# Waiting for gate/up weights one group earlier, and a bias matmul moved to the head of its block

## The reference, cut to what matters

```python
xn = layernorm(x)                                   # x: (2, 16384, 1024) f32
u  = einsum('bld,ed->ble', xn, W_in) + b_in         # D = 1024
h_t = exp(lambda_log) * h_{t-1} + gamma * u_t       # scan over blocks of 2048 rows
s  = einsum('bld,ed->ble', h, W_out) + b_out + xn
gate, up = xn @ (w_gate/127).T, xn @ (w_up/127).T   # hidden size 3072
f  = (silu(gate) * up) @ (w_down/127).T
out = x + s * silu(f)
```

## Time and profile before

| | us |
|---|---|
| runs of the kernel before, median (lowest, highest; 2 runs) | 1378.19 (1334.52, 1421.86) |
| the profiled execution's own time | 1338.26 |
| its span, slowest core (core 1) | 1336.7 |
| spans of the eight cores | 1326.8 to 1336.7 |
| TensorE matmuls busy, core 1 | 1288.7 (96% of the span) |
| VectorE, ScalarE, GpSimd busy | 354.6, 289.8, 193.8 |
| HBM traffic of the core over the span | 145 GB/s |

### The profile page before, as it was taken

One profiled execution on the slowest core, in us unless ns is written; L12 is line 12 of the kernel. 1 busy time (PEld: TensorE's weight loads), 2 busy tenths in 40 slices (PEclk: granted clock), 3 DMA queues, 4 the chain that ended last, 5 costly groups with the idle time before them and its releaser, 6 DMA issues.

```text
span 1336.7 us, 15889 instructions; the slowest of 8 cores (1326.8 to 1336.7 us)
## 1 busy us (share of the span) xinstructions
PE 1288.7 (96%) x6032; PEld 591.7 (44%) x6032; DVE 354.6 (27%) x566; ACT 289.8 (22%) x437; POOL 193.8 (14%) x198
## 2 busy tenths in 40 slices
PE   1899999999999999999999999999999999999997
PEld 1544445444444445444454444544445444444443
DVE  3222310334014240133302332033310434023322
ACT  3511023110231112211222112311023210231100
POOL 0100031300321004200133002130031200330002
PEclk9899999999999999999999999999999999999999
DMA  9964306773078411874028630566206741075201
GB/s 218 257 211 145 117 32 189 213 183 77 32 220 242 145 55 38 262 234 144 17 97 256 213 126 16 160 211 212 95 32 197 244 158 63 32 240 170 95 1 63
DMA packets 124798, 190.90 MB, mean 143 GB/s; under 512 B 3507, under 2 KB 101939, under 8 KB 124724
## 3 DMA queue, kind: packets, MB, share of 16 engines
q1 hardware_dynamic: 101524, 103.90, 25.6%
q0 software_dynamic: 23200, 85.99, 21.1%
HBM read 177.29 MB, written 16.78 MB: 145 GB/s over the span
## 4 chain that ended last, share of the span: by engine, by line
PE 91%; issue 5%; DMA 2%; ACT 1%; POOLq 1%; DVE 1%; ACTq 0%; POOL 0%; DVEq 0%
PE pb L343 25%; PE pb L297 24%; PE pb L305 24%; PE pb L322 9%; PE pb L274 6%; DMA winT<-win_t 2%; PE pb L255 2%; PE pb L327 2%; POOLq L61 1%; DVE hbT L470 0%; ACT xnb L236 0%; ACT gslab L358 0%; ACT gslab L401 0%; DVE xbuf L498 0%; DVE gslab L494 0%
## 5 line engine op out<-in xcount | busy, mean ns | idle before, releaser
L297 PE MATMUL pb<-xnbT,wgubuf 128*128 128x512 bf16 x1536 | 362.8, 379 | 6.5 <-DVE hbT L470 6.5
L305 PE MATMUL pb<-xnbT,wgubuf 128*128 128x512 bf16 x1536 | 362.8, 379 | 0.0
L343 PE MATMUL pb<-wdfull,hbT 128*128 128x512 bf16 x1536 | 332.9, 379 | 0.0
L470 DVE SCALAR_TENSOR_TENSOR hbT<-pb,gslab 128x512 bf16<-128x512 f32 x192 | 131.9, 690 | 564.2 <-PE pb L305 456.4
L297 PEld LDWEIGHTS pb<-xnbT,wgubuf 128*128 128x128 bf16 x1536 | 149.8, 98 | 189.2 <-issue 9.6
L401 ACT ACTIVATE gslab<-pb 128x512 bf16<-128x512 f32 x192 | 114.1, 598 | 541.6 <-PE pb L297 470.2
L305 PEld LDWEIGHTS pb<-xnbT,wgubuf 128*128 128x128 bf16 x1536 | 150.3, 98 | 181.2
L343 PEld LDWEIGHTS pb<-wdfull,hbT 128*128 128x128 bf16 x1536 | 149.7, 98 | 181.1 <-issue 1.8
L540 POOL TENSOR_TENSOR gslab<-gslab,s_sb 128x512 bf16<-128x512 bf16 x60 | 69.2, 1153 | 798.5 <-ACT gslab L358 792.0
L274 PE MATMUL pb<-xnbT,winT 128*128 128x512 bf16 (+1 forms) x576 | 122.6, 375 | 1.1 <-DMA winT<-win_t 1.1
L322 PE MATMUL pb<-woutT,guT 128*128 128x512 bf16 x512 | 121.5, 380 | 0.0
(11 more groups left out here) (29 smaller groups left out, 245.3 us busy)
## 6 DMA issues: line engine op xcount, KB each, us to landing
wgubuf<-wgu_t SPq DMA_DIRECT2D x96, 1024.0 KB, 6.4
wdfull<-wd_t POOLq DMA_DIRECT2D x32, 1536.0 KB, 18.2
out<-xbuf POOLq DMA_DIRECT2D x32, 512.0 KB, 3.0
xbuf<-xe POOLq DMA_DIRECT2D x7, 2048.0 KB, 12.4
winT<-win_t POOLq DMA_DIRECT2D x2, 1024.0 KB, 15.4
xbuf<-xe SPq DMA_DIRECT2D x1, 2048.0 KB, 19.4
woutT<-wout_t POOLq DMA_DIRECT2D x1, 2048.0 KB, 19.1
xbuf<-xe SPq DMA_DIRECT2D x2, 512.0 KB, 7.6
```

The lines of the kernel that those rows point to most:

```text
L297: O("tensor", lambda eng, g=g, cc=cc, kc=kc, gb=gb: eng.matmul(pb[gb][:, 0:512], wgubuf[g % 3][:, kc * 512 + cc * 128: kc * 512 + cc * 128 ...
L305: O("tensor", lambda eng, g=g, cc=cc, kc=kc, ub=ub: eng.matmul(pb[ub][:, 0:512], wgubuf[g % 3][:, kc * 512 + 256 + cc * 128: kc * 512 + 25 ...
L343: O("tensor", lambda eng, c=c, m=m, n=n: eng.matmul(pb[2 * m + n][:, 0:512], hbT[:, c * T + m * 128: c * T + m * 128 + 128], wdfull[:, c * ...
L470: O("vector", lambda eng, c=c: eng.scalar_tensor_tensor(hbT[:, c * T:(c + 1) * T], pb[3 + 2 * (c % 3)][:, 0:512], QINV, siluT[c % 2][:, :] ...
```

## The change

Two edits in `tensor_tile`. The wait for the weights is moved one group ahead: at the head of group `g` TensorE waits for the load of group `g+1`, and at group 0 for those of groups 0 and 1. The buffers, their number and the list of SyncE are unchanged. And in a block of the `W_out` product the bias matmul goes first and opens the accumulation; the last of the eight others closes it and bears the mark.

```diff
             for g in range(NGU):
                 G = (k - 1) * NGU + g
-                W("tensor", mark=("wgu", G))
+                if g == 0:
+                    W("tensor", mark=("wgu", G))
+                if g + 1 < NGU:
+                    W("tensor", mark=("wgu", G + 1))
                 for cc in range(2):
@@
                 if b >= 2:
                     W("tensor", mark=("sevac", k, b - 2))
+                O("tensor", lambda eng, b=b, n=n: eng.matmul(
+                    pb[b % 2][:, 0:512], ones_sb[0:1, :],
+                    bout_bf[0:1, n * 512:(n + 1) * 512],
+                    start=True, stop=False))
                 for kc in range(NK):
                     O("tensor", lambda eng, b=b, m=m, n=n, kc=kc: eng.matmul(
                         pb[b % 2][:, 0:512],
                         hTb[:, kc * T + m * 128: kc * T + m * 128 + 128],
                         woutT[:, kc * D + n * 512: kc * D + n * 512 + 512],
-                        start=(kc == 0), stop=False))
-                O("tensor", lambda eng, b=b, n=n: eng.matmul(
-                    pb[b % 2][:, 0:512], ones_sb[0:1, :],
-                    bout_bf[0:1, n * 512:(n + 1) * 512],
-                    start=False, stop=True),
-                    inc="s_t", mark=("S", k, b))
+                        start=False, stop=(kc == NK - 1)),
+                        inc=None if kc < NK - 1 else "s_t",
+                        mark=None if kc < NK - 1 else ("S", k, b))
```

## The result

| | kernel before | changed kernel |
|---|---|---|
| device time, median of all runs | 1336.84 (10 runs) | 1364.79 (11 runs) |
| ratio of the undisturbed runs | 1 | 1.0191, 95% interval 1.0161 to 1.0220 |

What follows compares the result with a forecast made beforehand. The prediction took TensorE's own matmul stream, without slack, to bound the kernel. To 1338.3 us it added 28 for the early wait, 4 for the clock and 0 for the bias matmul: 1370.3, said as 1370, range 1347 to 1385.

Steps and rivals of the forecast that it cites:

- the term for the early wait: At group heads, TensorE stops for weight loads over about 6.8 us: 28 us in all, bounds 15 and 45.
- The longest load of each tile less 6.9: Stops of a tile estimated as its longest weight load beyond one 6.9 us group: 28.4 us over core 1's tiles.
- if the loads themselves change much in duration: Sign that the prediction is wrong: the weight loads take a much different time to land; no size given.
- The bias matmul at 0: Moving the bias matmul within its `W_out` block costs 0, with bounds of 13.4 us gained or lost.
- The clock: TensorE runs at half clock behind long stops: two full prices of 2.1 us, 4 us taken, at most 10.5.
- The base of the sum: The profiled execution of the kernel before, 1338.3 us with a span of 1336.7, to which the terms were added.
- Slower by over 2%: Outcome for the whole kernel's time: above 1365 us, counted from 1338; chance 0.62.
- the case with 0.36: Outcome for the whole kernel's time: within 2% of the kernel before, not to be told from no change; chance 0.36.
- Stops stay short: Rival: the slowest core's weight-load stops are only 15 us, none over 3.0, and the clock holds: 1350; chance 0.30.
- Every long stop costs the clock: Rival: every long TensorE stop brings half clock, 10.5 us, and small excesses add: 1381; chance 0.14.
- Loads keep their durations: Rival: weight loads keep their old durations to the full, so stops come to 45 us: 1387; chance 0.05.
- The new place hides its weight loads: Rival: the bias matmul's new place in its block hides its exposed weight loads, 13 us less: 1357; chance 0.04.

Runs made afterwards that it cites:

- the edit alone: The kernel before with only the bias matmul moved to the head of its block, the wait left: ratio 0.9997.
- the wait alone: The kernel before with only the wait moved one group ahead, the bias matmul left at the end of its block: ratio 1.0181.
- the full rows: The kernel before with the bias matmul over 128 rows and not one, the others zero: ratio 0.9907.
- the run with eight long stops: The kernel before with one wait added a tile, at the head of group 8 for the load of group 10, issued at that moment: ratio 1.0501.

## Why the prediction was right and where it was off

**The step that failed: the size of the term for the early wait, and the base that it was added to.** "The longest load of each tile less 6.9", read from core 1 of before, was to put 28 us onto 1338.3. What the runs showed: stops of 24.7 us on the core that ended as the slowest of the undisturbed, 13.6 to 23.2 on the others, and this core had begun at 1327.5, not at 1336.7. With the clock the forecast added 32 us, and the change cost some 25. The details are below.

**What bounds the kernel, and the mechanism: right.** The stream of TensorE had no slack, each stop went into the time in full, and most signs that the prediction named are there: the new row in the waits, the half clock behind some long stops, no stop in tile 8 of core 5, 2.15 us a `W_out` block. One isn't: a group was to start within 0.1 us of its landing, and starts 0.35 us behind it. And one of the two signs of being wrong is there, "if the loads themselves change much in duration". That the early wait leaves a load one group where it had two is shown by the run with the wait in the middle of a group. That the long landing comes mostly from the input load is shown by the cut input load, for two thirds of the stops of tiles 2 to 7.

**The bias matmul at 0: right,** by the edit alone and by the unchanged 2.15 us. What the prediction left open, why the two loads are exposed, is now settled: the number of rows.

**The size of the stops: 3 us too many on core 5, as a sum of errors of both signs.** It took 28 us; core 5 has 24.7, the most of the undisturbed cores. Put onto core 5's own landings after the change, "longest less 6.9" gives 17.1 us, so three things are to be told apart.
- *The landings were shorter than those of core 1 of before: too many by 11.* The forecast kept durations. The prediction named a pull the other way, loads that are spaced further apart, and gave it nothing. In the three executions with the early wait (the changed kernel twice, the wait alone) the longest landings of tiles 2 to 7 have a mean of 8.4 us and none of 144 is over 10.6. In the four that have the wait where it was or half a group ahead, and the same transfers (before, the bias edit alone, the full rows, the wait in the middle), the means are 9.4 to 9.8, and 27 of 192 took 11 us or more. (The bias on VectorE, with one more transfer at the start, has 9.0 and three of 48.) That they shorten is thus shown; that the spacing does it is argued. Core 1 of before was the worst core of its execution, 28.4 us by "longest less 6.9" over the eight tiles, beside 23.0 on core 0 and 11.5 to 15.6 on the other six. The worst cores of the other three have 20 to 29, those of the three with the early wait 14 to 17.
- *The limit was too high: too few by 4.* It is 6.3 us and not 6.9, 0.6 for each of seven tiles.
- *Other loads of a tile add: too few by 3.* In tile 2 core 5 stopped twice, for 1.4 us each, in tile 7 for 1.8 and 2.1.

In tile 1, where the sum had 1.5 us, core 5 lost 5.6 and core 6 7.1. Its first load behind the start-up transfers took 8.4 us on core 1 of before, and I hadn't asked for the same load on the other cores: it took 10.5 us on core 5 and 10.7 on core 6.

**The clock: right in sum (4 us, measured 4.4 on core 5), wrong in its terms.** I expected five stops over 4 us and two full prices of 2.1. It was three stretches of about 1.5 us of loss, behind stops of 4.2, 3.0 and 3.5 us. The run with eight long stops puts the full price at 2.4 us on its core 0.

**The base of the sum: off.** The prediction added the stops to 1338.3, whose slowest core lost about 8 us (by group positions) in the second halves of groups waiting for VectorE (6.5 in the earlier trace rows). Some of that is no longer there to be added to: by group positions core 4 lost 3.6 us so before and core 7 lost 2.7, and neither loses anything after. (Core 2 goes the other way, from nothing to 1.5 us.) That a TensorE which has stopped for a load lets VectorE catch up would explain it and was not tested. And the largest growth fell on cores that had begun fastest: cores 2, 5 and 6, with 1326.8 to 1327.9 before, grew by 26.9 to 28.6 us; cores 3, 4 and 7, with 1332.5 to 1333.6, by 11.3 to 18.2. Why it fell so stays open. 1356 is the outcome of a core that began at 1327.5.

**The time and the chances.** 1370 was said and 1364.79 measured (median; the undisturbed runs lie between 1355.7 and 1367.3), inside the range of 1347 to 1385. "Slower by over 2%" had 0.62, and the ratio of 1.0191, with an interval to 1.0220, lies within 2%: the case with 0.36. The forecast's own range of 1358 to 1378 was drawn around a sum 5 to 10 us too high, and that was enough to cross the bound. The figure was also made against the profiled execution only. Against the table's median of two runs, 1378.19, the same 1370 reads as a small gain, the opposite of what the text argues. The text named the run of 1422 behind that median, but didn't say which way the forecast lies from it; eight more runs put it at 1336.84.

**The rivals.** "Stops stay short" (1350) was nearer than its chance of 0.30 suggests: three of the six undisturbed cores had under 18 us. "Every long stop costs the clock" falls as a price for this kernel, for want of long stops (one of 7.1 us, on core 6, and it did cost the clock), but holds as a mechanism. "Loads keep their durations" is refuted by the landings. "The new place hides its weight loads" is refuted by the edit alone.

## What to carry to other kernels

With n buffers and loads that go out when a buffer comes free, a load has n-1 steps until it is needed; a wait placed one step early takes one of them away, and a first price can be read beforehand as the landings longer than what is left. What was left here is 6.3 us of a step of 6.9, and the landings themselves got shorter once the wait had moved, so such a price is rough both ways. Read it on all cores and in all stages, not on the slowest core of one execution: which core is slowest may change with the edit. And where an operand with one row stands between operands with 128, look at the gaps between the weight loads: making it full-sized, or moving it to an idle engine, was worth 0.9% and 2.0% here, while moving it inside its block was worth nothing.

## What the runs showed of the hardware that I had not expected

- A group starts 0.35 to 0.39 us behind the landing that it waits for, in all fifteen such stops of core 5.
- A weight load with half the bytes beside a 2 MB input load still took 10.9 us to land on core 1 in tile 2, where the loads behind it took 3.6. In the later tiles none took over 7.5.
- The longest landings of a tile got shorter with the early wait: a mean of 8.4 us against 9.4 to 9.8 with the same transfers.
- A stop of 3.3 us was followed by a half clock until 920.5 us; all eight stops of 5.5 us and more on core 0 of the run made for it were, at 2.4 us each beyond the stop itself.
- Two weight loads around a single-row matmul are exposed, about 0.1 us each; over 128 rows, none is.
